# Another order of the steps of a period in a software-pipelined perceiver block

## The reference

```python
x = x + xattn(layernorm(x), ctx, ...)  # 16 heads of 128; keys and values from 257 context rows of 128; rmsnorm on q and k
x = x + attn(layernorm(x), ...)        # causal, 16 query heads, 4 key heads of 16; rmsnorm, rope, ternary weights
x = x + moe(layernorm(x), ...)         # top 1 of 8 experts with a capacity of 256 rows, plus a shared expert
```

## Time and profile before

| what | value |
|---|---|
| median of 3 runs | 1457.01 us (1456.34 to 1458.7) |
| profiled execution, its span | 1457.0 us |
| a period without a fall of the clock | 75.85 us |
| a period with one | 77.18 us |
| PE busy | 1274.8 us (87%) |
| DVE, ACT, POOL busy | 916.5, 892.3, 541.9 us |

### The profile page before, as it was taken

One profiled execution on the slowest core, in us unless ns is written; L12 is line 12 of the kernel. 1 busy time (PEld: TensorE's weight loads), 2 busy tenths in 40 slices (PEclk: granted clock), 3 DMA queues, 4 the chain that ended last, 5 costly groups with the idle time before them and its releaser, 6 DMA issues.

```text
span 1457.0 us, 34962 instructions
## 1 busy us (share of the span) xinstructions
PE 1274.8 (87%) x10526; PEld 856.9 (59%) x10526; DVE 916.5 (63%) x3300; ACT 892.3 (61%) x3736; POOL 541.9 (37%) x1337
## 2 busy tenths in 40 slices
PE   5777999999999999999999999999999999846781
PEld 2554666666666666666656566666666666535661
DVE  6744767677676767676767676767666776631212
ACT  4455676767675757585767677676767676611330
POOL 2044252626262534344353525252526262400004
PEclk9998999999999999999999999999999999956986
DMA  9100000101010101010000000000101011003434
GB/s 372 42 23 12 21 23 11 33 11 34 11 33 11 34 11 33 7 34 11 26 18 23 22 17 28 16 22 15 29 11 33 11 33 69 6 1 106 142 112 130
DMA packets 41183, 59.58 MB, mean 41 GB/s; under 512 B 5094, under 2 KB 35953, under 8 KB 40096
## 3 DMA queue, kind: packets, MB, share of 16 engines
q1 hardware_dynamic: 36880, 50.73, 10.9%
q0 software_dynamic: 2064, 6.14, 1.3%
q10 hardware_dynamic: 2176, 2.10, 0.4%
HBM read 48.62 MB, written 10.49 MB: 41 GB/s over the span
## 4 chain that ended last, share of the span: by engine, by line
PE 51%; DVE 16%; issue 8%; ACT 8%; POOL 5%; DMA 3%; POOLq 0%; SPq 0%; DVEq 0%; ACTq 0%
PE AB L603 25%; PE Db L603 9%; PE Eb L603 7%; DVE kst L1345 3%; PE C L603 3%; DVE rq L1402 2%; DMA ctxn<-expert_rows 2%; PE C L728 2%; PE C L743 2%; POOL prob L1202 2%; ACT AB L961 1%; ACT prob L1031 1%; DVE pT L1529 1%; DVE px L1611 1%; ACT wt_q L953 1%
## 5 line engine op out<-in xcount | busy, mean ns | idle before, releaser
L961 ACT ACTIVATE AB<-AB 128x128 f32<-128x128 f32 (+1 forms) x1160 | 304.9, 263 | 108.2 <-PE AB L603 105.1
L1157 POOL TENSOR_TENSOR pjunk<-pjunk 128x1 f32<-128x1 f32 x288 | 57.1, 198 | 681.4 <-DVE sinv L1524 387.0
L1345 DVE BATCH_NORM_STATS2 kst<-AB 128x6 f32<-128x256 f32 x512 | 181.7, 417 | 110.1 <-PE AB L603 110.1
L603 PE MATMUL AB<-wk_hi,c_hi 128*128 128x512 f16 x512 | 199.7, 390 | 21.8 <-POOL c_lo L1163 10.0
L961 ACT ACTIVATION_READ_ACCUMULATOR AB<-AB 128x1 f32 (+1 forms) x1160 | 218.1, 188 | 0.0
L603 PE MATMUL AB<-wk_lo,c_hi 128*128 128x512 f16 x512 | 197.8, 386 | 0.0
L603 PE MATMUL AB<-wk_hi,c_lo 128*128 128x512 f16 x512 | 197.3, 385 | 0.0
L1031 ACT ACTIVATE prob<-prob,nbias,rq 128x257 f32<-128x257 f32 x256 | 150.7, 593 | 8.0 <-DVE nbias L1519 8.0
L1202 POOL TENSOR_SCALAR prob<-prob,sinv 128x257 f32<-128x257 f32 x256 | 129.9, 507 | 20.2
L603 PE MATMUL AB<-ctxT,qpT 128*128 128x257 f32 x512 | 123.2, 383 | 11.4 <-ACT pxT L1063 11.4
L603 PEld LDWEIGHTS AB<-wk_hi,c_hi 128*128 128x128 f16 x512 | 50.9, 99 | 103.7 <-issue 32.5
(11 more groups left out here) (270 smaller groups left out, 2853.7 us busy)
## 6 DMA issues: line engine op xcount, KB each, us to landing
ctxT<-in_ctxT SPq DMA_DIRECT2D x64, 128.5 KB, 2.1
ctxn<-in_ctxn SPq DMA_DIRECT2D x64, 128.0 KB, 2.1
wq_hi<-in_w SPq DMA_DIRECT2D x4, 768.0 KB, 5.0
wq_lo<-in_w SPq DMA_DIRECT2D x4, 768.0 KB, 6.6
expert_rows<-base POOLq DMA_DIRECT2D x1, 2048.0 KB, 15.6
xin<-in_x SPq DMA_DIRECT2D x16, 128.0 KB, 2.2
prob<-in_wqT SPq DMA_DIRECT2D x1, 2048.0 KB, 19.3
xres<-in_x SPq DMA_DIRECT2D x16, 128.0 KB, 2.0
```

The costliest lines, as they stand in the source:

```text
L603: return pe.matmul(out, lhsT, rhs, start=start, stop=stop)
L961: ins = nc.scalar.activation(k, k, ACT.Square, accum_out=sums[0:m, h:h + 1])
L1157: own.mark(pool.tensor_tensor(pjunk[:, 0:1], pjunk[:, 1:2], pjunk[:, 1:2], ALU.mult))
L1345: ins = V.bn_stats(stats[:, 0, 2 * half + n], AB[0:m, 2 + half, 2 * D * n:2 * D * (n + 1)])
```

## The change

The four lists of `ORDER` are written in another order; the prologue's lists, the operations and the buffers stay, but for the scratch of the roots, which becomes one tile for each root (`cube`). The diff of one list, and of the scratch:

```diff
-    "PE": """K0 pt3 K1 X K2 o3 K3 f Q xt1 K4 qkv QP rk0 s0 qk sc rk1 K5 K6 K7 pt0 pv s1 st pr rk2 s2 o0 xt2 rk3
-              lg up s3 pt1 dn pos o1 pt2 o2""".split(),
+    "PE": """K0 K1 pt3 X K2 o3 K3 f Q xt1 rk0 K4 qkv QP s0 qk sc rk1 K5 K6 K7 pt0 pv s1 st pr rk2 s2 rk3 xt2 o0 lg up
+              s3 pt1 dn pos o1 pt2 o2""".split(),
...
-        nc_ = sb("nc_", [P, NB * H])
+        cube = {n: sb(f"cube_{n}", [P, k]) for n, k in (("KN0", NB * H), ("KN1", NB * H), ("RQ", H), ("qkv", NQK))}
...
-                w, c = guess[name][:], nc_[:, 0:guess[name].shape[1]]
+                w, c = guess[name][:], cube[name][:]
```

More of the change, by code:

```diff
@@ L149 @@
 ORDER = {
-    "PE": """K0 pt3 K1 X K2 o3 K3 f Q xt1 K4 qkv QP rk0 s0 qk sc rk1 K5 K6 K7 pt0 pv s1 st pr rk2 s2 o0 xt2 rk3
-              lg up s3 pt1 dn pos o1 pt2 o2""".split(),
[L152 to L156, removed]
+    "PE": """K0 K1 pt3 X K2 o3 K3 f Q xt1 rk0 K4 qkv QP s0 qk sc rk1 K5 K6 K7 pt0 pv s1 st pr rk2 s2 rk3 xt2 o0 lg up
+              s3 pt1 dn pos o1 pt2 o2""".split(),
+    "ACT": """K0 K1 tl3 X ph3 K2 oh3 K3 gKN0 Q xt1 gRQ K4 qkv rk0 gqkv QP qk e0 rk1 K5 sc K6 K7 ph0 tl0 gKN1 pv rk2 e1
+              rk3 xt2 oh0 up e2 ph1 tl1 lg e3 oh1 ph2 tl2 oh2""".split(),
+    "DVE": """K0 X K1 XL dp3 K2 K3 do3 KN0 kn0 f Q RQ K4 qkv rq qr s0 sc K5 i0 sm K6 K7 KN1 dp0 kn1 ys yv s1 pr ln2 s2
+              i1 lg do0 up i2 s3 dn dp1 pos i3 do1 dp2 do2""".split(),
+    "POOL": """h0 h1 n3 X c3 c1 h2 h3 r0 r1 ln1 cl n0 r2 c0 y r3 ln2 c2 n1 n2 scat""".split(),
 }
@@ L1307, in newton @@
                 for r in range(3):
-                    c = nc_[0:rows, 0:n]
+                    c = cube["KN1"][0:rows, 0:n]
                     step(V.scalar_tensor_tensor(c, w, -0.5, w, ALU.mult, ALU.mult))
```

## The result

The changed kernel takes 1502.14 us, median of 4 runs (1499.70 to 1504.72), where the kernel before, run on the same chip, takes 1457.12 (1456.34 to 1458.70). The ratio is 1.0309, with a 95% interval of 1.0295 to 1.0324: slower by 45 us. The profiled execution has a span of 1494.2 us. It was granted 0.945 of the clock on average; the timed ones, with spans of 1497.9 to 1502.9 us, 0.941 to 0.943. In which stretch they had less can't be seen, as only the profiled one has a trace.

The account below looks back on a forecast made before the run. PE, busy 87% of the span, was taken to bound the kernel. Terms: 15 x 1.45 + 15 x 0.46 - 14 x 0.15 = 26.6 us, plus 8.0 for the clock, on 1457: 1491 us, range 1470 to 1504.

Parts of the forecast that it names:

- heads: rk0 before K4 and qkv before rq make qk start later: a loss of 1.45 us a period, bounds 0.88 and 1.67.
- tl0: This ACT copy, moved ahead of gKN1 and pv's copies, delays s1: a loss of 0.46 us a period, bounds 0 and 0.56.
- rk3, xt2, o0: Reordering these steps exchanges equal work whose inputs are there: no effect.
- K1 before pt3: K1 on PE gives POOL's n3 time to finish, so PE's wait before pt3 goes: -0.54 us a period.
- i2 before s3: On DVE i2 waits for e2, delaying s3, dn, e3, pos, scat, h0 and finally K0: some 0.4 us a period.
- the end of the loop: The pt3 gain and the i2 delay together: a gain of 0.15 us a period, bounds -0.9 and +0.4.
- the absorbed case: Rival: something else holds the chain to K5, so the heads' delay costs nothing; 1462 or 1457 us, chance 0.05.
- c3 behind X: POOL waits there for o3, but its 8.5 us of idle time until kn0 holds the four splits: no effect.
- the scratch: A scratch tile for each root, on one engine in its own order: no effect.
- Clock: The longer lull between s0 and K5 brings 11 falls instead of five, 1.33 us each: a loss of 8 us in all.
- the clock falls in every period: Rival: the lull before K5 lets no period escape, 15 falls, ten more than now, 13.3 us: 1497 us, chance 0.2.
- My main case: The forecast itself: 11 clock falls in fifteen periods, 1491 us, chance 0.72.

Follow-up runs that it names:

- e4: The changed kernel with seven unused products of 512 columns added on PE behind s0 in each full period; 1490.47 us.
- e3: The changed kernel with rk0 back behind QP on PE and ACT, and rq back before qkv on DVE; 1469.53 us.
- e6: The kernel before with K1 ahead of pt3 on PE and of tl3 on ACT, and h1 ahead of n3 on POOL; 1447.97 us.
- e12: e3 with i2 behind s3 and i3 behind dp2 on DVE again, as in the kernel before; 1457.84 us.
- e9: e4 with five more unused products behind qk in each full period; 1479.37 us.
- e10: The kernel before with one unused product of 512 columns behind s0 and five behind qk in each full period; 1450.23 us.
- e8: e6 with qkv ahead of K4 on PE, ACT and DVE, and rk0 ahead of qkv on PE; 1435.90 us.
- e11: e8 with five unused products of 512 columns behind qk in each full period; 1440.05 us.

## Why the prediction was right

Forecast: 1491 us, in a range of 1470 to 1504. Measured: 1502.14, slower, inside the range and near its upper end. The terms, per full period at full clock:

| term | predicted | measured | from |
|---|---|---|---|
| heads | +1.45 | +1.35 | e4 less e3 |
| tl0 | +0.46 | +0.27 | step at s1, e6 to e12 |
| rk3, xt2, o0 | 0 | +0.21 | step at lg, e6 to e12 |
| K1 before pt3 | -0.54 | -0.55 | e6 less before |
| i2 before s3 | +0.4 | +0.42 | e3 less e12 |
| sum | 1.77 | 1.70 | e4 less before: 77.55 - 75.85 |

The measured terms are differences along one chain, before, e6, e12, e3, e4, with the step from e6 to e12 split by the rows; they add up by construction, and what speaks for each is its own pair of runs. The recorded sum has 1.76, as it rounds the two parts at the end of the loop to -0.15. Two other slips of the prediction change little: 1457.0 + 34.6 is 1491.6, and the absorbed case without tl0 is 1455, not 1457.

**Heads: right, step by step.** PE's idle time before qk was to be 1.67 us and is 1.55, DVE's wait before `vals` 1.1 and is 1.02, the wait for the guess is gone. The shift of 1.38 at qk is passed on nearly whole (1.35), as said: the absorbed case is out.

**tl0: right mechanism, mis-sized.** I moved pv by the full 0.46 between tl0's start and gKN1's. The extra at s1 is 0.27. From start to start gKN1 came 633.38 - 632.22 = 1.16 us behind ph0 in the trace before; now tl0 comes 652.12 - 651.17 = 0.95 behind ph0 and gKN1 0.48 behind tl0, which is 0.27 more. So tl0 starts 0.2 ahead of gKN1's old place, not 0.1, and holds up gKN1 for 0.48, not 0.56.

**"Exchanges of equal work whose inputs are there: nothing": this step failed**, by 0.21. xt2's input is there, but its copy on ACT was put behind rk3's, and lg needs the copy. I looked at PE's side of the exchange only.

**End of the loop: the size held, the way did not.** K1's gain is the 0.54 read from start to start. The loss of 0.4 was to travel over pos, scat and h0 to K0. It travels by dn: late by more than the 0.2 I gave it, it holds o1 on PE. `c_lo` costs 0.7 in either order. That 0.4 came out was luck: it is not the chain that I had added up. In the sum the 0.19 too much for tl0 and the 0.21 missed at lg cancel as well.

**c3 behind X, and the scratch: nothing, as said.** POOL's cover was used and was enough. For the scratch no run stands alone; e12 has it and e6 has not, and PE's steps shift nowhere between them but at s1 and lg.

**Clock: the rival's count, and a larger price.** I took 11 falls at 1.33 us; all fourteen full periods fall. Against the 77.57 us of e9 eleven of them lose 1.41 on average and three 2.57, 23.2 in all, where the five before lost 6.8. In the three the low clock lasts well into K5. So the clock adds 16.4 us in the profiled execution instead of 8.0, the order 14 x 1.72 = 24.1, and the stretch behind the fourteen, in which the clock falls in both kernels, 0.8: to 0.1 the 41.2 us of the loop. The other 4 us between this and the 45 of the medians lie in executions without a trace and aren't accounted for; the start is a candidate, as the profiled execution has the shortest of all traces, 142.3 us to the first f (last section).

The rival "the clock falls in every period" gave 1497 and was the case that came true; given its count, its price of 1.33 a fall was what fell short. My main case, eleven falls, did not occur. That 1502 is inside the range is in part luck: the upper end of 1504 was this rival with 7.7 us more at the end of the loop, which did not come; falls dearer than I had put them, and those 4 us, filled that room instead.

The Trainium skill, TensorE: Matmul & The Clock Gate, Part 4 (PE-mode transpose), says that turns don't count as activity as matmuls do; by that rule I had called this rival the likelier case, and it was. Ordinary products put in between stopped the falls (e9, e10). They also filled waits in which PE had stood idle, and no run replaces the turns alone, so the runs fit the rule but don't isolate it.

## What to carry to other kernels

Where engines take their steps in a fixed order, cost a moved step by who waits for the step behind it, and follow it through every engine that it has a part on: an idle 1.1 us on DVE, or a copy on ACT put behind another, came out on PE as the price. On an engine whose clock falls in a lull, a delay that lengthens the lull is paid twice, here 24 us for the order and 16 for the clock; unused products in the lull tell the two apart, one run for each kernel. The latest input of the step where the bottleneck waits is the one to bring forward: with qkv ahead of K4, and K1 ahead of pt3, the kernel before gained 21 us (9 with K1 alone), where the change lost 45.

## What the runs showed of the hardware that I had not expected

**The length of the lull doesn't set the number of falls by itself.** Before, e6, e12 and e3 have the same PE order from s0 to K5, and a lull of 4.56 us; they show 5, 2, 4 and 7 falls with periods of 75.85, 75.30, 75.78 and 76.20 us. In e4 4.4 us are left behind the filling, and ten of fourteen fall, with 77.55. In this set the falls grow with the period, one execution each; e6, with two falls in its trace, was timed at 1441.81 to 1454.16 us with a granted clock of 0.960 to 0.954, so its count may well be another in another execution. The Trainium skill, TensorE: Matmul & The Clock Gate, Part 1 (The HAM clock gate), says that what the gate watches runs freely and is not started by a kernel, by which the period would decide how the lull falls upon it; these counts fit that, and no run tests it.

**A prologue of the same instructions takes 142.3 to 147.5 us**, by the first f of each trace. Windows from 20 to 40 us, of e8 (first f at 142.7) and of e11 (146.8):

```profile
20.00:40.00 20.00, 14.09 (x66) 5.84 (x65) 15.66 (x45) 13.36 (x69) 1.08 (x2) 1.00 1.01 407
```

```profile
20.00:40.00 20.00, 14.19 (x53) 5.22 (x53) 14.87 (x43) 13.34 (x65) 1.18 (x2) 0.83 1.02 404
```

Where the clock is low there, PE gets through fewer instructions, and the start is some 4 us later. Behind the last f e11 needs 172.8 us and e8 169.0. From first to last f the two agree to 0.2 us (1121.2 and 1121.4). From the traces a difference of 4 us between two of these kernels is therefore better read in the periods than in the total.
